# Expert routing over 32 token tiles as thirteen whole-width VectorE instructions instead of 384 per-tile ones

## What is computed

```python
xn = layernorm(x)
# attention branch: 16 heads of 64, softmax over ALL keys, masked only afterwards
s = (where(causal, softmax(Q @ K.T / 8), 0) @ V)
# mixture-of-experts attention branch
logits = normalize(xn) @ normalize(sim, axis=0) - sigmoid(gates)     # [tokens, 8]
gated  = relu(logits)
mask   = gated > 0;  where no expert is active: the top 2 of logits
rw     = softmax(where(mask, gated, -1e9))
q, k, v = sum_e mask[:, e] * (xn @ proj[e])                          # D = 128
f = causal_softmax(q @ k.T / sqrt(128)) @ v
g = silu(sum_e (mask * rw)[:, e] * (f @ o_proj[e]))
out = x + s * g
```

## Time and profile before

| what | us |
|---|---|
| median of 2 runs | 3755.8 (3736.71 and 3774.89) |
| profiled execution, its own time | 3775.85 |
| its span on core 3, the slowest | 3774.3 |
| PE, DVE, ACT busy in that span | 2624.5, 2334.9, 2124.5 |
| spans of the 8 cores | 3714.5 to 3774.3 |

### The profile page before, as it was taken

One profiled execution on the slowest core, in us unless ns is written; L12 is line 12 of the kernel. 1 busy time (PEld: TensorE's weight loads), 2 busy tenths in 40 slices (PEclk: granted clock), 3 DMA queues, 4 the chain that ended last, 5 costly groups with the idle time before them and its releaser, 6 DMA issues.

```text
span 3774.3 us, 60465 instructions; the slowest of 8 cores (3714.5 to 3774.3 us)
## 1 busy us (share of the span) xinstructions
PE 2624.5 (70%) x18642; PEld 1172.8 (31%) x18642; DVE 2334.9 (62%) x6261; ACT 2124.5 (56%) x2466; POOL 255.4 (7%) x706
## 2 busy tenths in 40 slices
PE   1103799975765887787778777788777777776552
PEld 1101344432332333333333333333333333333220
DVE  4435766631433667667767766766766776776665
ACT  0000000035110779779878977976977886898662
POOL 0010000000000001000000100100100010010112
PEclk9997888878997887787787688678777768866555
DMA  2240000001122000000000000000000000002445
GB/s 89 78 124 21 1 1 1 1 1 41 50 85 105 3 3 7 4 4 4 7 4 4 7 3 4 7 4 3 6 5 4 4 7 3 4 9 69 137 137 194
DMA packets 35781, 117.15 MB, mean 31 GB/s; under 512 B 5778, under 2 KB 5778, under 8 KB 35474
## 3 DMA queue, kind: packets, MB, share of 16 engines
q1 hardware_dynamic: 22738, 71.34, 5.6%
q0 software_dynamic: 12736, 41.95, 3.7%
HBM read 79.72 MB, written 33.55 MB: 30 GB/s over the span
## 4 chain that ended last, share of the span: by engine, by line
PE 41%; ACT 20%; issue 13%; DVE 12%; DMA 9%; DVEq 4%; POOL 0%; ACTq 0%; SPq 0%; POOLq 0%
PE PB L680 10%; ACT expC L1330 6%; ACT stagef L1345 6%; PE PB L880 5%; PE PB L894 5%; DMA stagef<-x 4%; PE PB L865 4%; PE PB L794 4%; PE PB L797 3%; PE PB L752 3%; ACT stagef L1330 3%; PE PB L809 3%; ACT R L1345 2%; DVE tmpc L1194 2%; DVEq L1262 1%
## 5 line engine op out<-in xcount | busy, mean ns | idle before, releaser
L1194 DVE TENSOR_REDUCE tmpc<-stagef 128x2 f32<-128x1024 bf16 (+2 forms) x726 | 811.5, 1127 | 238.9 <-ACT stagef L1345 180.6
L1330 ACT ACTIVATE expC<-PB 128x1024 bf16<-128x1024 f32 x768 | 859.1, 1119 | 88.6 <-PE PB L880 88.6
L1345 ACT ACTIVATE stagef<-PB 128x1024 bf16<-128x1024 f32 x600 | 672.6, 1121 | 202.3 <-PE PB L894 131.2
L1194 DVE TENSOR_REDUCE tmpc<-R 128x2 f32<-128x1024 bf16 (+2 forms) x362 | 406.1, 1122 | 117.8 <-ACT R L1345 89.0
L1330 ACT ACTIVATE stagef<-PB 128x1024 bf16<-128x1024 f32 x384 | 432.4, 1126 | 73.5 <-PE PB L880 73.5
L880 PE MATMUL PB<-R 64*128 64x512 bf16 x1152 | 296.2, 502 | 234.1 <-ACT stagef L1345 137.3
L680 PE MATMUL PB<-R,xnT 128*128 128x512 bf16 x1536 | 397.2, 428 | 72.0 <-DVE qk_tmp L1070 71.1
L880 PE MATMUL PB<-QTt,KTt 64*128 64x512 bf16 x1152 | 286.7, 486 | 144.0 <-ACT stagef L1345 77.9
L1345 ACT ACTIVATE R<-PB 128x1024 bf16<-128x1024 f32 x296 | 332.1, 1122 | 83.9 <-PE PB L894 59.7
L1310 ACT ACTIVATE expC<-PB 128x512 bf16<-128x512 f32 x144 | 84.1, 597 | 454.3 <-PE PB L720 452.5
L894 PE MATMUL PB<-R 64*128 64x512 bf16 (+3 forms) x1088 | 261.4, 472 | 40.3 <-ACT expC L1330 21.7
(11 more groups left out here) (161 smaller groups left out, 3035.6 us busy)
## 6 DMA issues: line engine op xcount, KB each, us to landing
stagef<-x SPq DMA_DIRECT2D x64, 512.0 KB, 4.3
out<-Vau SPq DMA_DIRECT2D x32, 512.0 KB, 3.5
g_sp<-stagef SPq DMA_DIRECT2D x32, 256.0 KB, 2.0
s_sp<-s_stage POOLq DMA_DIRECT2D x64, 128.0 KB, 2.4
QTt<-g_sp POOLq DMA_DIRECT2D x32, 256.0 KB, 5.7
KTt<-s_sp POOLq DMA_DIRECT2D x32, 256.0 KB, 5.8
R<-qp POOLq DMA_DIRECT2D x8, 512.0 KB, 5.1
R<-kp POOLq DMA_DIRECT2D x8, 512.0 KB, 4.6
```

What stands on the lines that cost most here:

```text
L1194: e.tensor_reduce(s.tmpc[:].rearrange("p (h c) -> p h c", h=2)[:, :, c:c + 1], s.c1scr((m1 - 1) % 3)[:, 0:2 * kw] .rearrange("p (h k) -> p ...
L1330: e.activation(s.expCs(es), PB[[0, 1, 3][it["slot"]]][:, :], AF.Exp).then_inc(sem["aC2"], 1)
L1345: e.activation(scr[:, 0:1024], pbsrc[:, 0:1024], AF.Exp).then_inc(sem["aC1"], 1)
```

## The change

Routing is computed for all 32 tiles at once. Each tensor of 128 x 256 is seen as 128 x 32 x 8 (tile, expert). The column for each tile (`invr_all`, the maxima, the reciprocal) is read with a stride of 0 over the 8 experts, the gate values with a stride of 0 over the 32 tiles. Intermediate values go into 128 x 256 and 128 x 32 tensors that are free at this point (`mq_all`, `rwp_all`, `expg_all`, `lna`, `lnv`, `ddt`). The values computed are the same. The second loop (L1026) becomes one instruction with the reciprocal's column repeated, and a drain behind it.

```diff
-            for qt in range(NT):
-                lg = s.lnat[:, qt * 8:(qt + 1) * 8]
-                e.tensor_scalar(s.rt1[:], lg, s.invr_all[:, qt:qt + 1], None, ALU.mult)
-                e.drain()
-                e.tensor_tensor(s.rt2[:], s.rt1[:], s.sgb[:], ALU.subtract)
-                e.drain()
-                e.reduce_max(s.rtm[:, 0:1], s.rt2[:], axis=AX.X)
...
-                e.scalar_tensor_tensor(s.msk_all[:, qt * 8:(qt + 1) * 8], s.rt4[:],
-                                       s.rti[:], s.rt5[:], ALU.mult, ALU.add)
-                e.tensor_scalar(s.gated_all[:, qt * 8:(qt + 1) * 8], s.rt2[:], 0.0,
-                                None, ALU.max)
+            A3 = lambda t: t[:].rearrange("p (q ee) -> p q ee", ee=8)
+            bcq = lambda t: bass.AP(t, 0, [[32, 128], [1, 32], [0, 8]])
+            sgb_b = bass.AP(s.sgb, 0, [[8, 128], [0, 32], [1, 8]])
+            e.tensor_tensor(A3(s.mq_all), A3(s.lnat), bcq(s.invr_all), ALU.mult)
+            e.drain()
+            e.tensor_tensor(A3(s.rwp_all), A3(s.mq_all), sgb_b, ALU.subtract)
+            e.drain()
+            e.tensor_reduce(s.lna[:], A3(s.rwp_all), AX.X, ALU.max)
+            e.drain()
+            e.tensor_tensor(A3(s.mq_all), A3(s.rwp_all), bcq(s.lna), ALU.is_ge)
+            e.drain()
+            e.scalar_tensor_tensor(A3(s.expg_all), A3(s.mq_all), -1.0e9,
+                                   A3(s.rwp_all), ALU.mult, ALU.add)
+            e.drain()
+            e.tensor_reduce(s.lnv[:], A3(s.expg_all), AX.X, ALU.max)
+            e.drain()
+            e.tensor_tensor(A3(s.expg_all), A3(s.rwp_all), bcq(s.lnv), ALU.is_ge)
+            e.tensor_scalar(s.ddt[:], s.lna[:], 0.0, None, ALU.is_le)
+            e.drain()
+            e.tensor_scalar(s.mq_all[:], s.rwp_all[:], 0.0, None, ALU.is_gt)
+            e.tensor_tensor(A3(s.gated_all), A3(s.expg_all), bcq(s.ddt), ALU.mult)
+            e.drain()
+            e.tensor_tensor(s.msk_all[:], s.gated_all[:], s.mq_all[:], ALU.add)
+            e.drain()
+            e.tensor_scalar(s.gated_all[:], s.rwp_all[:], 0.0, None, ALU.max)
...
-            for qt in range(NT):
-                e.tensor_scalar(s.rw_all[:, qt * 8:(qt + 1) * 8],
-                                s.rwn_all[:, qt * 8:(qt + 1) * 8],
-                                s.Zi_all[:, qt:qt + 1], None, ALU.mult)
+            bcq2 = lambda t: bass.AP(t, 0, [[32, 128], [1, 32], [0, 8]])
+            e.tensor_tensor(s.rw_all[:].rearrange("p (q ee) -> p q ee", ee=8),
+                            s.rwn_all[:].rearrange("p (q ee) -> p q ee", ee=8),
+                            bcq2(s.Zi_all), ALU.mult)
+            e.drain()
```

## The result

The changed kernel takes 3654.6 us, the median of 11 runs (3646.78 to 3708.26), against 3742.2 us for the kernel before, the median of 10 (3734.33 to 3812.5). The ratio is 0.9761, 95% interval 0.9734 to 0.9787: 2.4% faster. The forecast was 1.94%, at 3683 us, with 3650 to 3713 as its range and 0.45 on a gain of over 2%. So the direction and the range held, while the gain is 14.6 us larger than the 73 us forecast (3742.2 - 3654.6 = 87.6). The prediction had given "same" 0.53 and "faster" 0.45, so of the two sides of the 2% threshold it had held the one that came for slightly less likely.

What follows compares the result with a forecast made beforehand. DVE's routing was taken to hold PE 71.1 us before the projections. 71.1 us plus 3.05 for the clock, less 1.6, gave 72.5 us; about 73 off the 3755.8 us median gave 3683 us, range 3650 to 3713.

Steps and rivals of the forecast that it cites:

- The path: Before the projections, DVE's routing work holds PE; batching it saves DVE 71.7 us, of which 71.1 us are kept.
- PE takes over without a gap: At the end of projection tile 0, PE becomes the bound by 0.6 us and goes on at 329.1 us.
- SCALAR_TENSOR_TENSOR and stride-0 operands at the dense price: In the new routing chain, SCALAR_TENSOR_TENSOR takes 0.5 us and repeated operands cost what dense ones do.
- The second term: At projection tile 1, PE's clock no longer falls to 0.50 after the pause: 3.05 us saved.
- third rival: The same as "DVE remains the bound"; there PE's clock is perhaps down for the 3.05 us.
- The third term: In core 3's projection stage, the roughly 50 us full-clock spell starts earlier, before 0.81: 1.6 us lost.
- Nothing else is late: Behind the q sums no other work delays PE; DVE is busy only 226.93 of 330 us in the projection stage.
- the first two terms: Around projection tiles 0 and 1, PE's removed wait (71.1 us) and its held clock (3.05 us): together 74.1 us.
- The clock takes more back: Without the rest, PE's clock is 0.81 from projection tile 1 on; gain only 62.3 us; chance 0.16.
- Fewer cores fall: In the projection stage all cores stay at clock 1.00 in more executions; median 3663 us; chance 0.12.
- DVE remains the bound: The new routing chain takes 10 us instead of 5.2, so PE still waits 4.2 us; gain 67 us; chance 0.07.
- Slower: In the later attention stage the clock falls below 0.76; at 0.70 the kernel is 73 us slower; chance 0.03.

Runs made afterwards that it cites:

- rest_8x: Changed kernel with eight reductions over 128x8192 (69.9 us of DVE work) added behind routing; ratio to the kernel before 0.9966, median 3721.63 us.
- loop1_only: Changed kernel with its second loop (L1026) left as before, only the routing loop batched; ratio to the kernel before 0.9788, median 3656.78 us.
- loop2_only: Kernel before with only its second loop replaced by one instruction, the routing loop kept; ratio to the kernel before 0.9991.
- after_again: The changed kernel measured again, nothing altered; median 3650.24 us, ratio to the kernel before 0.9789.
- after_third: The changed kernel profiled a third time, nothing altered; 3643.61 us.
- before_again: The kernel before with a second profile, nothing altered; 3740.76 us.
- small_at_end_x3: Changed kernel with 1056 small tensor_scalar instructions and 768 drains appended at the end of DVE's stream; 3914.42 us.
- rest_quarter: Changed kernel with one reduction over 128x2048 (2.3 us) added on DVE behind routing; 516.4 us from logits copy to first output projection matmul.
- rest_1half: Changed kernel with one reduction over 128x4096 (4.4 us) added on DVE behind routing; 519.3 us from logits copy to first output projection matmul.

## Why the prediction was right, and where it missed

*The path.* Right. DVE's work before the q sums held PE. DVE saves 72.0 us (71.7 forecast); the chain up to the last routing instruction takes 319.08 - 313.99 = 5.1 us (5.2 forecast). rest_8x puts the time back with other work on DVE and brings the stage from 510.4 to 584.6 us, and loop1_only and loop2_only divide the gain of the stage as forecast within 2 us.

*PE takes over without a gap.* Right where tile 0 is slow, by about the 0.6 us forecast or less: on core 0 DVE ended q at 325.84 us, and PE went straight on. It hangs on the clock at the beginning of tile 0. On three cores of after_again and one of after_third tile 0 ran at full clock (10.3 to 10.5 us instead of some 12), and there PE waits 1.24 us for q. There is next to no slack: of the 3.8 us of the second loop 2.5 to 3.3 come back as a wait on cores 3 and 0 of loop1_only.

*SCALAR_TENSOR_TENSOR and stride-0 operands at the dense price.* Right, 0.43 us each; the upper bounds (0.70 us, and double) were far off.

*The second term, the clock after the pause: 3.05 us.* Right in kind: 13.32 against 10.52, 2.8 us, on core 3 of before_again. The forecast set 13.41 us from the timeline against 10.36 from the chain; with the timeline's 10.52 for both it would have been 2.9. A wait of 2 to 4 us can cost nearly as much as one of 70, which the prediction had only as a "perhaps" in its third rival.

*The third term, -1.6 us, and the two executions.* This is the step that failed. The prediction took the 0.81 on cores 2 and 3 as part of the kernel, with a full-clock spell of some 50 us that would be spent earlier, and the median of 3755.8 as the middle of two kinds of executions of which it would meet one each. The second profile of before has no 0.81, small_at_end_x3 has it without a pause. The before's median over 10 runs is 3742.2. For the usual execution the term should have been nothing; what it is in one with the 0.81 stays open.

*Nothing else is late.* Not so. The prediction read DVE's 226.93 us of 330 as slack and called PE the bound of the stage. But in the timeline DVE's instructions follow one another without idle time and take 10.6 us for a tile, against PE's 10.47. The distance from tile to tile, as PE's transposes (L665) mark it on core 3, is 10.47 us for 12 tiles in before_again and then 10.6 to 10.9; after (after_third) it is 10.47 for 3 tiles and then 10.6. I read this as a lead that DVE has on PE after a slow tile 1 and loses by 0.1 us a tile: loop1_only, with a slow tile 1 on core 3, has 10.47 for 16 tiles, and core 3 of rest_quarter, with a fast one, for none. Most of the tiles of 10.9 us have one of DVE's gaps of 0.46 us in them or just ahead of them, and the changed kernel has neither. Over all tiles it is 321.3 us against 322.6 on core 3, 1.3 us in favour of the change (1.8 in the mean of the cores), that no step of the prediction has. That the shorter lead and the missing gaps nearly cancel is luck.

*The sum.* By the table, with the mean of the two last columns: start -6.1, stage -76.7, next piece -1.4, pairs -6.1. The stage is 4.2 us more than the 72.5 forecast. In the mean of the cores 73.6 us come up to the first L665, where the first two terms had 74.1, 1.8 in the tiles and 1.3 behind the last L665. The start and the pairs together are 12 us that the prediction did not have, and most of the 14.6 us by which the gain was missed. The start goes with the load times of x, whose cause is open. For the pairs I have no cause: from the first L794 to the end the variants lie at 2603.4 (after_third), 2605.6 (rest_8x), 2607.8 (loop2_only), 2609.9 (loop1_only) and 2610.4 us (rest_1half), so the differences are within what kernels with the same pairs show; it stays open.

*The rivals.* "The clock takes more back" (62 us) did not come, and in most executions there is no 0.81 for it to act on; in small_at_end_x3, where there is, it held from tile 0 on, much as this rival has it. "Fewer cores fall" named a time near the right one, 3663 against 3654.6 us, by another way: it took the kernel before for one with fallen cores in every other execution, while its median of 3742.2 is already that of executions without them (before_again: 3740.76). "DVE remains the bound" was priced for a chain of 10 us and missed for this reason, but DVE does set the pace from tile 4 on, and loop1_only shows how little is needed to bring PE's wait back. "Slower" (the pairs' clock) did not happen. On core 0 after, 1200 to 3400 us:

```profile
1200.00:3400.00 2200.00, 1689.59 (x13420) 753.21 (x13492) 1542.48 (x3878) 1779.47 (x2004) 174.73 (x529) 0.75 0.03 10
```

0.75 as in the earlier trace rows.

## What to carry to other kernels

A loop of small vector instructions costs by their number: 352 of them over 8 elements took 73 us, 12 over 256 elements 5 us, and an operand repeated with a stride of 0 cost nothing extra. Whether that is worth anything is read from the wait it ends: here PE had run ahead of the loop by one tile and then had nothing to do for 71 us. A busy share of two thirds is no slack where the instructions already follow one another without a gap: compare the engine's time for one round with the other engine's. And before a clock level is put into a sum, look at a second profile: one execution can have an event that the kernel doesn't own.

## What the runs showed of the hardware that was not expected

- A short wait can cost about as much clock as a long one: tile 1 took 13.05 us after 4.1 us, 12.98 after 68.9 us, 12.21 after 2.0 us. It need not: it took 10.52 (nothing) after 1.2 to 1.6 us, after 2.0 us on another core of the same execution, and after 3.3 us on core 0 of loop1_only.
- In this stage the 0.81 came to a pair of cores (2 and 3, in two profiles of different kernels), not to their die.
- DVE had 9 to 12 idle gaps of 0.46 us among identical instructions in some programs and none in others, nearly the same number on each core (10 or 11 in the kernel before, none after), 26 or 53 us apart. The cause is open.
- 32 loads of 512 KB each took 3.4 to 3.9 us by program and execution, with identical instructions around them: up to 12 us at the start of a kernel.
